# One layer of local attention and a routed feed-forward: TensorE's column-half groups put together

## The reference

```python
qkv = x @ W_attn + b_attn                     # 256 -> 3 * 256; 16 heads of 16
scores = einsum('bhtd,bhsd->bhts', q, k) / 4
mask = (j <= i) & (j >= i - 64)               # each token sees itself and 64 before it
x = layernorm(x + (softmax(where(mask, scores, -inf)) @ v) @ W_proj + b_proj)

expert_idx = argmax(softmax(x @ Wr.T))        # one of 8 experts for each token
inter = gelu(x @ W1[expert_idx] + b1[expert_idx])    # 256 -> 1024, exact gelu
y = inter @ Wo + bo + x
x = layernorm(x + gamma * normalise(y) + beta)
```

## Time and profile before

| what | value |
|---|---|
| three runs | 534.67, 536.47, 536.82 us; median 536.47 |
| the profiled execution: its own time | 537.07 us |
| its span from first to last instruction | 535.3 us |
| TensorE busy | 491.7 us, 92% |
| TensorE loading weights | 434.6 us, 81% |
| VectorE busy | 427.2 us, 80% |
| ScalarE busy | 351.9 us, 66% |
| GpSimd busy | 317.7 us, 59% |
| mean granted TensorE clock | 0.976 |

### The profile page before, as it was taken

The page is one execution under the profiler, slowest core; times in us unless marked ns, Lnnn a source line. Parts: engine busy times, 40 slices in busy tenths (PEclk is TensorE's granted clock), DMA queues, the critical chain, the costliest instruction groups (busy, mean ns, idle before and its releaser), DMA issues. The chain is left out here.

```text
span 535.3 us, 24509 instructions
## 1 busy us (share of the span) xinstructions
PE 491.7 (92%) x8576; PEld 434.6 (81%) x8576; DVE 427.2 (80%) x1122; ACT 351.9 (66%) x793; POOL 317.7 (59%) x559
## 2 busy tenths in 40 slices
PE   7799999998999999999977898899999999999980
PEld 6588888877888888888866687788999999999970
DVE  5437978877888888888788647999999989999882
ACT  6246786856686777768676665565676666767850
POOL 8303264535354545546454447777888888888773
PEclk9969999989999999999999899999999999999996
DMA  7797777776877867797762121222235564542100
GB/s 188 210 240 194 216 188 195 206 215 157 216 211 212 234 184 214 210 249 204 199 177 78 52 71 52 71 72 67 66 104 168 194 206 158 170 144 72 50 23 8
DMA packets 90296, 82.28 MB, mean 154 GB/s; under 512 B 36534, under 2 KB 83903, under 8 KB 90050
## 3 DMA queue, kind: packets, MB, share of 16 engines
q1 hardware_dynamic: 86832, 72.26, 49.5%
q0 software_dynamic: 3248, 8.41, 4.6%
q10 hardware_dynamic: 98, 0.04, 0.0%
HBM read 43.50 MB, written 23.55 MB: 125 GB/s over the span
## 5 line engine op out<-in xcount | busy, mean ns | idle before, releaser
L1409 PE MATMUL ps<-v_even,w_hi 128*128 128x128 f16 x1024 | 140.5, 219 | 0.8 <-issue 0.8
L1391 PE MATMUL ps<-wo_hi,ks 128*128 128x256 f16 (+1 forms) x576 | 128.6, 273 | 8.1 <-DVE ks L1087 7.2
L830 ACT ACTIVATE probs<-ps,b1T 128x128 f32<-128x128 f32 (+1 forms) x312 | 85.5, 360 | 67.1 <-PE ps L1409 63.8
L1409 PE MATMUL ps<-v_even,w_lo 128*128 128x128 f16 x512 | 107.9, 219 | 0.0
L1409 PEld LDWEIGHTS ps<-v_even,w_hi 128*128 x1024 | 96.6, 98 | 3.4 <-issue 1.4
L1158 DVE TENSOR_REDUCE mx<-ps 128x4 bf16<-128x512 f32 x128 | 82.6, 683 | 11.9 <-PE ps L1460 11.6
L740 POOL CAST att_hi<-att 128x256 f16<-128x256 f32 x32 | 12.6, 394 | 112.8 <-DVE att L1225 112.8
L1391 PE MATMUL ps<-wo_lo,ks 128*128 128x256 f16 (+1 forms) x288 | 78.5, 273 | 0.0
L1087 DVE TENSOR_TENSOR ks<-probs,ks 128x512 f16<-128x512 f32 (+1 forms) x72 | 69.7, 967 | 8.5 <-ACT ks L837 5.0
L849 ACT ACTIVATE probs<-ps 128x512 f32<-128x512 f32 x128 | 69.5, 611 | 6.7 <-PE ps L1486 3.8
L1509 PE MATMUL ps<-v_odd,probs 128*64 128x17 f32 x1024 | 69.9, 210 | 0.8 <-issue 0.6
(11 more groups left out here) (247 smaller groups left out, 1280.9 us busy)
## 6 DMA issues: line engine op xcount, KB each, us to landing
qk_s<-qk_room SPq DMA_DIRECT2D x32, 256.0 KB, 2.8
w_in<-in_L_ffn_W_dram SPq DMA_DIRECT2D x16, 512.0 KB, 5.7
v_odd<-slots SPq DMA_DIRECT2D x64, 128.0 KB
qs<-qk_s SPq DMA_DIRECT2D x16, 384.0 KB
ks<-qk_s SPq DMA_DIRECT2D x16, 384.0 KB, 5.5
ks<-qk_s SPq DMA_DIRECT2D x32, 144.0 KB
v_even<-v_odd SPq DMA_DIRECT2D x63, 68.0 KB, 3.2
qk_s<-qk_room SPq DMA_DIRECT2D x32, 128.0 KB, 3.0
```

Source lines behind the costliest of these rows:

```text
L830: last = nc.scalar.activation(g[1 - p][:, ic, n * w:(n + 1) * w], ps_h[1 - p][:, half, col + n * w:col + (n + 1) * w], ACT.Gelu, bias=b1T[ ...
L1391: ins = mm(ps_y[p][0:m], h[p][hs][:, ic, 0:m], wo[ws][:, ic, :], start=n == 0, stop=n == 3 * IC - 1)
L1409: up_ins = mm(ps_h[1 - p][:, half, col + m * w:col + (m + 1) * w], weights(ws, m, k, ic), sT[1 - p][ss][:, k, at], start=k + n == 0, stop= ...
```

## The change

Five things are changed, all in the attention loop.

1. TensorE's order in a pass: the projection and the turn of x come first, then scores 0 and 1, directly ahead of the values. In pass 0 the scores still come first. `mx` and its turned copy are 128 wide instead of 32; ScalarE reads the same 32 rows of it.
2. The turned x goes to bank 4, where it waits for the exponential that reads that bank, and no longer for the q/k parts. The rank products go to bank 6 (but for the last pair) and lose their waits for the v copy and the router term; the wait for `place_done` moves from the projection to the values.
3. On ScalarE the copy of v stands behind the maxima's rows.
4. On VectorE y and logits come ahead of maxima 0 and 1; the router term comes behind the copy of attT, and the places of the tokens ahead of the w1 split.
5. The two halves of a w1 unit are split in the even pass, and none in the odd one.

```diff
-        mx = [sb(f"mx{k}", [P, P - ALIGNED], bf16) for k in range(2)]
+        mx = [sb(f"mx{k}", [P, P], bf16) for k in range(2)]
         def ps_x(t):
-            return ps[:, 0 if t >= LEAD else 4 + t % 2, 0:CC * P]...
+            return ps[:, 4 if t >= LEAD else 4 + t % 2, 0:CC * P]...
-        ps_rank = ps[:, 1, 320:320 + 3 * E]...
+        def ps_rank(pair):
+            return ps[:, 6 if pair < TILES // 2 - 1 else 1, 320:320 + 3 * E]...
-        ps_mx = ps[0:P - ALIGNED, 2, 0:P]...
+        ps_mx = ps[:, 2, 0:P]...
         def w1_halves(it):
-            halves_at = range(it - 1, it) if it < TILES - 3 else ...
+            halves_at = range(it - 2, it if it % 2 == 0 else it - 2) if it < TILES - 3 else ...
# TensorE, in values(0)
+                        wait(pe, place_done, (done - 1) // 2)
# TensorE, the pass
                 if it == 0:
                     warm(20)
-                scores(0)
+                    scores(0)
+                    scores(1)
                 if a_tile(old):
                     ...
-                    wait(pe, place_done, old // 2)
                     product(ps_proj, ...).then_inc(proj_done, 1)
-                scores(1)
                 for t in turned(it):
                     ...
                     if t >= LEAD:
-                        pe.wait_ge(qkh_done, t)
-                        pe.wait_ge(qkl_done, t)
+                        wait(pe, exp_done, 4 * (it - 1) + 1)
                     ...
+                if it != 0:
+                    scores(0)
+                    scores(1)
                 values(0)
```

53 lines of the change are left out of this document (26 added, 27 removed).

## The result

The kernel after takes 543.19 us in the median (20 runs, 537.22 to 553.97), the kernel before beside it 538.56 (20 runs, 533.59 to 546.83): ratio 1.0063, 95% interval 1.0032 to 1.0093, slower by 0.6%. I had forecast 527, faster. The profiled execution of the kernel after took 541.54 us (span 539.8, mean granted clock 0.945), that of before 537.07 (535.3, 0.976).

A forecast was written before the change was run, and what follows sets the result against it. TensorE's pace bounds the attention loop, VectorE close behind. Thirteen tile pairs gain 0.83 us each (10.8), w_out tiles give back 1.2: sum -9.6, so 527 us from a median of 536.47; range 519.5 to 536.5.

The forecast's parts named there:

- TensorE's own time: TensorE's floor per tile: falls 0.57 us, from 8.27 to 7.70 in odd tiles and 8.16 to 7.59 in even ones.
- the stalls: Between undisturbed passes: 0.4 us of the 8.64 mean gap per tile, in some tiles only, no engine named as cause.
- the clock: TensorE's granted clock: 1.00 in the stretch read, new waits only 0.2 us, so a fall to half clock got no chance.
- Six changes of width: TensorE's column-width switches: eight a tile become two, each costing 0.09 to 0.12 us, taken as 0.095.
- the rank products: Odd tiles on TensorE: four matmuls at 0.03 us each, so even tiles, without them, have a floor of about 8.16.
- The loops bind: Loops through ScalarE and VectorE set the period, 7.80 us in odd and 7.89 in even tiles; chance 0.52, 527 us.
- The rival that TensorE stays the bound: Both loops shorter than TensorE's floor, so 0.57 us comes free in all 30 tiles: 17 us, 519.4; chance 0.15.
- y and logits ahead of the first maxima: VectorE: delays the first maxima by 0.49 us, for which the third scores group waits; costed at nothing, 0.2 a tile if late.
- the v copy: On ScalarE behind the maxima's rows: 2 us later for SP, whose v_even loads start well after it; costed at nothing.
- The gap with no cause in my evidence: TensorE's stall of 0.27 us before 196.51, inside the values line L1509, with no engine named as cause.
- The slower rival: Even tile's VectorE chain: attT starting beyond +3.01 loses what odd tiles gain; at +3.4, 541.5 us; chance 0.15.
- The transfers: Second key windows (L485) have 1.3 us of slack; if missing in most pairs, gain shrinks to 0 to 3, 535; chance 0.18.

The follow-up runs named there:

- e1: Kernel after with y and logits put back behind the first two maxima and x's low part; 537.41 us, ratio 1.0073 to before.
- e3: Kernel before with only TensorE's order, the 128-wide mx and the banks with their waits changed; 536.46 us, ratio 1.0023 to before.
- g4: Kernel after with 31 more 8x8 transposes in the first pass, where TensorE idles; 538.49 us, ratio 1.0074 to before.
- f4: Kernel before with mx and its turned copy 128 wide and nothing else; 539.38 us, ratio 1.0029 to before.
- e7: Kernel before with w1 loads from the third unit on cut to 1/16 of the columns; 529.56 us, ratio 0.9932 to before.
- f1: Kernel after with two idle transposes at the x turn of each pass, ahead of the scores; 543.91 us, ratio 1.0111 to before.
- h1: Kernel before with the fourth scores group of eight passes waiting for the third group's maxima, which it does not need; 557.70 us, ratio 1.0363.
- e8: Kernel before with only the late v copy, VectorE's new order and both w1 halves in even passes; 541.68 us, ratio 1.0161.
- e6: Kernel after with w1 loads from the third unit on cut to 1/16 of the columns; 535.49 us, ratio 0.9997 to before.

## Why the prediction was wrong

TensorE's own time fell as forecast. Two other steps failed: the stalls, which I let stay as they were, and the clock, to which I gave no chance of its own.

*TensorE's own time: right.* Six changes of width at 0.095 less are 0.57; by the ledger it is 0.64 to 0.74 a pass in after, 0.62 to 0.65 in e1, e3 and g4, and 0.19 for the two changes of f4. The odd pass came out at 7.73 against 7.80. One term was wrong and cost little: I gave the rank products 0.11 in odd passes, where they take 0.03 (e7: 8.16 and 8.13).

*The loops bind: right.* f1 adds 0.44 us of TensorE work and the short pass stays at 7.73. The rival that TensorE stays the bound is out for odd passes.

*y and logits ahead of the first maxima, "I cost it at nothing": mis-sized.* I looked at odd tiles, where it holds. In every even tile the first maxima come late. TensorE's third scores group starts 0.2 us late for them, in some tiles 0.3 to 1.1, and VectorE then idles for that group, here in pass 12, which lasts 8.18 where the sum has 7.89:

```profile
141.84 1.29 DVE L1160 TENSOR_REDUCE mx<-ps 128x4 bf16<-128x512 f32 x2 [0.27 <-PE ps L1462]
```

The q/k low part started at +3.97, near where I had put it (+3.92); what follows it took 4.2 us, where the sum has 3.97. In the even tiles that split w_out it is worse. VectorE, kernel after, against the earlier trace rows:

```profile
188.43 0.42 DVE L1265 COPY attT<-ps 128x512 f16<-128x512 f16 x1 [1.14 <-PE ps L1627]
189.00 0.17 DVE L1182 TENSOR_TENSOR lx<-ps,lb 128x8 f32<-128x8 f32 x1
189.08 1.28 DVE L1174 SCALAR_TENSOR_TENSOR w_lo<-w_in,w_hi 128x512 f16<-128x512 f32 x2
190.28 0.68 DVE L1292 SCALAR_TENSOR_TENSOR qk_room<-ps,qk_room 128x512 f16<-128x512 f32 x1
190.88 0.98 DVE L1318 SCALAR_TENSOR_TENSOR wo_lo<-w_lo,wo_hi 128x512 f16<-128x512 f32 x1
191.79 0.41 DVE L1188 SCALAR_TENSOR_TENSOR y<-ps,wa_in 128x256 f32<-128x256 f32 x1
192.13 0.15 DVE L1192 TENSOR_TENSOR logits<-ps,lx 128x8 f32<-128x8 f32 x1
192.20 1.27 DVE L1160 TENSOR_REDUCE mx<-ps 128x4 bf16<-128x512 f32 x2
```

and TensorE, which waits for the first of them:

```profile
193.02 0.64 PE L1462 MATMUL ps<-ks,qs 112*64 112x128 f16 x16 [0.93 <-DVE mx L1160]
```

The second w1 half (0.60), the w_out part (it stood there before as well), y and logits (0.41) all stand ahead of the first maxima, and the router term started 0.2 late behind the v copy that I had moved in thought for SP only. The wait is 0.93 where I had 0.2 at most. The period of such a pass, 8.49 in my sum, is 9.0 to 9.4 in three and 10.8 in the one that half clock follows: some 2 us, and the half clock behind two of them (after 157.62 and 209.80) besides. But e1, which takes the order back and has even passes of 7.82 to 7.88, is no faster: the step is wrong in size, not the cause of the sign.

*"The other 0.4 us of the mean are stalls", and stay: wrong, and one of the two steps that fail the forecast.* I summed undisturbed passes and let the gaps between them be what they were. The sum itself gives back 5.2 us of the 14.8 that TensorE's own time falls in passes 2 to 27, as waits on ScalarE and VectorE. The gaps grew by 11.1, from 9.1 to 20.2 us: the waits just named, those for ScalarE, and the loads of instructions. Those loads were already in the trace of before, at 116.27 and 131.38, outside the stretch I had read, and I did not ask what a faster TensorE does to them. The gap with no cause in my evidence is not one of them. It comes back in pass 20,

```profile
213.35 0.18 PE L1509 MATMUL ps<-v_even,probs 128*64 128x17 f32 x1 [0.25 <-issue]
```

356 matmuls later, which is exactly two passes and no multiple of 124; f4 and h1 have it at the same two places, to within one matmul. Smaller ones of 0.27 to 0.34 stand near that place in most even passes of before. They are gone in e7 (lighter transfers) and in e8 (VectorE's and ScalarE's order of after); what they are stays open.

*The clock, "I give it no chance of its own": the other step that fails the forecast, and the one that gives the sign.* I took the clock of 1.00 in the earlier trace rows as safe since its gaps were small, and my own new waits as 0.2 us. The new waits were 0.9. The Trainium skill, TensorE: Matmul & The Clock Gate, section HAM oscillation — how this bites in real kernels, says that idle gaps bring the half clock back. Its example has waits of some 3 to 5 us; h1 shows it here with gaps of 0.9 to 1.6 us in a TensorE that is otherwise busy, and the measurement decides. After's clock is 0.953 in the median; before's was 0.964 to 0.970 in the five later groups. The slope over the 20 runs of after is 4.1 us for 0.01 (correlation -0.85; 2.7 without the five longest), so 0.011 to 0.017 are 3 to 7 us, about the 3.4 to 4.6 by which after is slower. At equal clock the two kernels would be roughly level; that estimate rests on a line through runs, not on an experiment. g4, the same kernel, is 4 us slower at 0.957 against 0.964, of which the slope gives 2 to 3. So of the 14 us between the forecast gain of 9.6 and the measured loss, by this estimate the clock took 3 to 7; the gaps took another 5 to 8 (19.6 to 22.4 us in e1, e3, g4 and after, against the 9.2 of before and the 5.2 of the sum).

*The slower rival* (attT in even tiles beyond +3.0) is not what happened: attT starts at 188.43 = +2.10. The transfers are not late either: no wait for ks stands in the list of 40 to 270 us, and e6 and e7 gain alike.

**What stays open.** No run takes both kinds of gap out of after without adding work, so how the loss divides between gaps and clock is an estimate. Further open: why only one gap in three brings the half clock, and which; whether fewer instructions would take the loading gaps away; whether a long run of narrow groups adds to the loss of clock; and the part of h1's cost beyond its gaps and its clock.

## What to carry to other kernels

A floor taken from undisturbed passes is a floor, not a forecast: work out what else the faster engine will run into, above all its instruction supply and the next engine's chain in the passes that carry extra work. Where TensorE is nearly always busy, a new wait near 1 us can cost about twice its length, as in h1, since the clock may halve behind it; put into the sum each such wait with its price, and look at the granted clock over all runs, not at one execution. An idle time without a named cause wants a test of its own before it is called noise, or given the cause of another: shifting the program by a few instructions told in one run whether it belongs to the work or to the stream.

## What the runs showed of the hardware that I had not expected

- Gaps of 0.9 to 1.6 us, eight in 270 us, took the mean clock from 0.964 to 0.944 and cost twice their length (h1). Over 18 kernels the clock falls with the number of such gaps.
- TensorE's instructions come in packets of 16 KB, one for some 124 matmuls; at some of the boundaries it stands for 0.3 to 1.7 us, in a place that depends on the count of instructions alone (after and g4). The gaps of after end 2.3 to 2.9 us after a packet's start.
- A change of column width costs some 0.1 us also by the whole loop: two less a pass took 0.19 us from TensorE's own steps (f4), six less 0.62 to 0.74 (e1, e3, g4, after).
